# A selective-scan block on one core: norm statistics, softplus passes and the z product in other steps, and GpSimd's four B products at states 5, 7, 9, 11

## What is computed

```python
x = x + mamba(ln_channels(x))       # x: 4 x 512 x 24 x 24; pixel shuffle: 128 channels, 2304 positions
# inside, per image, after a projection to u, z (256 channels each), a causal 4-tap conv and silu on u:
dt, Bm, Cm = split(x_proj @ u);  dt = softplus(dt_proj @ dt + bias);  A = -exp(A_log)
h = exp(dt * A) * h + (dt * u) * B   # 256 channels x 16 states, one position after the other
y = sum_over_states(h * C) + u * D
y = out_proj @ (y * silu(z))
t = tokens(x)                        # then a layer norm over the 512 channels of each token (ln_t)
t = t + ffn(ln_t(t))                 # ffn: tokens 1..128 replaced by a routed mix of memory tokens
```

## Time and profile before

| | us |
|---|---|
| median of 3 runs | 1271.66 (1270.97 to 1273.31) |
| profiled execution, its own time | 1275.06 |
| its span, first to last instruction | 1273.2 |
| POOL busy | 1107.9 (87%) |
| PE busy | 1095.4 (86%) |
| DVE busy | 1088.3 (85%) |
| ACT busy | 874.4 (69%) |
| mean granted PE clock | 0.935 |

### The profile page before, as it was taken

One profiled execution on the slowest core, in us unless ns is written; L12 is line 12 of the kernel. 1 busy time (PEld: TensorE's weight loads), 2 busy tenths in 40 slices (PEclk: granted clock), 3 DMA queues, 4 the chain that ended last, 5 costly groups with the idle time before them and its releaser, 6 DMA issues.

```text
span 1273.2 us, 13359 instructions
## 1 busy us (share of the span) xinstructions
PE 1095.4 (86%) x3786; PEld 646.5 (51%) x3786; DVE 1088.3 (85%) x1269; ACT 874.4 (69%) x1628; POOL 1107.9 (87%) x753
## 2 busy tenths in 40 slices
PE   6578888898898898898988988988988988989797
PEld 4334554555555555455555555555555555555344
DVE  1298999998999999998998999999989999999772
ACT  2466777767767757767767767777668677687543
POOL 4188999998999999998999989999989999999763
PEclk8678999998999999998999989999989999999898
DMA  6221213212213212222213212222122132232561
GB/s 163 76 74 52 101 60 103 101 58 106 102 57 106 97 62 90 92 82 82 101 58 105 101 58 99 76 88 101 60 104 101 57 106 101 75 105 93 172 207 37
DMA packets 64539, 116.80 MB, mean 92 GB/s; under 512 B 34218, under 2 KB 47954, under 8 KB 64466
## 3 DMA queue, kind: packets, MB, share of 16 engines
...
## 4 chain that ended last, share of the span: by engine, by line
POOL 31%; PE 21%; issue 18%; ACT 17%; DVE 12%; POOLq 0%; DMA 0%; DVEq 0%; SPq 0%; ACTq 0%
POOL SCAN L427 18%; DVE SCAN L1008 9%; PE Yp L736 7%; POOL SCAN L439 7%; PE PP L891 4%; ACT DA L504 3%; POOL GZ L418 2%; DVE SCAN L968 2%; PE PP L819 2%; PE PP L871 2%; ACT GATES L618 2%; ACT GATES L537 2%; ACT GATES L534 2%; ACT GATES L619 1%; PE PP L864 1%
## 5 line engine op out<-in xcount | busy, mean ns | idle before, releaser
L1008 DVE TENSOR_TENSOR_SCAN SCAN<-DA,CAR,SCAN 128x384 f32<-128x384 f32 x768 | 728.7, 999 | 67.4 <-ACT DA L504 34.4
L427 POOL TENSOR_TENSOR SCAN<-SCAN,CS 128x768 f32<-128x768 f32 x384 | 692.6, 1820 | 36.6 <-DVE SCAN L1008 32.0
L736 PE MATMUL Yp<-SCAN,IDENT 128*128 128x384 f32 x1536 | 588.6, 510 | 54.8 <-DVE VV L979 38.5
L504 ACT ACTIVATE DA<-UDT,A 128x384 f32<-128x384 f32 x768 | 432.3, 578 | 218.6 <-DVE SCAN L1008 215.1
L736 PEld LDWEIGHTS Yp<-SCAN,IDENT 128*128 128x128 f32 x1536 | 288.9, 198 | 267.0 <-POOL SCAN L427 104.7
L968 DVE TENSOR_TENSOR SCAN<-UDT,BB 128x768 f32<-128x768 f32 x288 | 269.3, 935 | 34.8 <-PE BB L718 34.8
L439 POOL TENSOR_TENSOR SCAN<-UDT,BS 128x768 f32<-128x768 f32 x96 | 175.3, 1826 | 0.0
L891 PE MATMUL PP<-XN,WT 128*128 128x384 f32 x384 | 141.1, 503 | 0.0
L891 PEld LDWEIGHTS PP<-XN,WT 128*128 128x128 f32 x384 | 77.3, 202 | 56.7 <-issue 11.0
L718 PE MATMUL BB<-PT,SEL 96*128 96x384 bf16 x288 | 98.7, 343 | 2.4 <-DVE SCAN L968 2.3
L451 POOL TENSOR_TENSOR UDT<-UDT 128x768 f32<-128x768 f32 x24 | 43.5, 1812 | 48.3 <-DVE UDT L1085 48.3
...
## 6 DMA issues: line engine op xcount, KB each, us to landing
...
```

What stands on the lines that cost most here:

```text
L427: pool.tensor_tensor(M[:, n1 % MRING], HB[:, n1 % HRING], over_halves(CS[:, n1 % CRING]), ALU.mult).then_inc(m_ready, 1)
L504: act.activation(DA[:, h, 0:T], DT[:, par, h], ACT.Exp, scale=A[:, h, n:n + 1])\
L736: last = pe.matmul(Yp[:, h, 0:T], IDENT[:, :], M[:, n3 % MRING, h], start=n3 == 0, stop=n3 == NS - 1)
L1008: dve.tensor_tensor_scan(HB[:, s % HRING, h], DA[:, h, 0:T], HB[:, s % HRING, h], CAR[:, ds(J * NS * HALVES + s * HALVES + h, 1)], ALU.mul ...
```

## The change

It moves pieces to other steps, on five engines; no piece is added or dropped, no tile changes its size.

- GpSimd's driving terms are those of states 5, 7, 9, 11 in place of 3, 5, 7, 9. State 3 goes to PE and DVE, state 11 to POOL. The DMA that fills BS now waits for the last of POOL's four products of the unit before.
- Back norm: mean and XC2 from steps 9/10 to 6 (XC2 behind the scan of the step), square from 11 to 7, variance from 12 to 9, its Ln/Exp from 12 to 10, POOL's two instructions from 13/14 to 12/13.
- Norm of unit J+3: square from 11 to 10, variance from 12 to 11, Ln/Exp from 12 to 11.
- Softplus: Exp in step 7, Ln and Exp in 8, two squares in 9, Identity in 10, the other two squares in 11, and all of them behind the decays of their step.
- z: product from step 10 to 12 (in the units without norm it stays at 10), its two readings from 11 to 12, the clamp from 12 to 13. u*D (L742) from step 11 to 10.

```diff
-POOL_STATES = (3, 5, 7, 9)
+POOL_STATES = (5, 7, 9, 11)
...
                 sp.wait_ge(rows_written, 16 * (unit + 1))
+                positive(sp, dbu_pool, NPOOL * unit)
...
-                if main and s == 12:
+                if main and s == 13:
                     pool.wait_ge(sgz_chain, 2 * J + 1)
...
-                if front and s == 10:
-                    act.wait_ge(fac_chain, 3 * f + 2)
-                    act.activation(SS[:, :, :], SS[:, :, :], ACT.Square, bias=FITB[:, 2:3], scale=FIT_S)\
-                        .then_inc(fac1_square, 1)
...
                     act.activation(DT[:, fp], PPT, ACT.Relu).then_inc(relu_done, 1)
-                if front and s == 8:
                     act.wait_ge(sp_chain, 3 * f + 1)
                     act.activation(SE[:, :, :], SE[:, :, :], ACT.Exp, scale=-1.0).then_inc(sp_chain, 1)
+                if front and s == 8:
                     act.wait_ge(sp_chain, 3 * f + 2)
...
-                if main and s == 11:
+                if main and s == (12 if norm else 11):
                     act.wait_ge(z_ready, J + 1)
...
-                if back and s == 11:
+                if back and s == 7:
                     act.wait_ge(xc2_ready, k + 1)
...
-                if back and s == 9:
+                if back and s == 6:
                     pe.wait_ge(x2_ready, k + 1)
-                    if front:
-                        pe.wait_ge(relu_done, f + 1)
                     for q in range(Q):
                         last = pe.matmul(STAT2, MEANW[:, :], unit_x(k)[:, q], start=q == 0, stop=q == Q - 1)
...
+                if main and s == (12 if norm else 10):
+                    if back:
+                        pe.wait_ge(ln2_done, k + 1)
+                    if front:
+                        pe.wait_ge(relu_done, f + 1)
+                    if norm:
+                        pe.wait_ge(ln_done, g + 1)
...
                     pe.wait_ge(hi_ready, f + 1)
                     if back:
-                        pe.wait_ge(x2_ready, k + 1)
+                        pe.wait_ge(xc2_ready, k + 1)
```

102 lines of the change are left out of this document (49 added, 53 removed).

## The result

The changed kernel takes 1278.57 us (median of 6, 1277.19 to 1280.50) where the kernel before takes 1273.39 (6 runs, 1270.97 to 1276.27): a ratio of 1.0033, 95% interval 1.0017 to 1.0050 (the two medians by themselves give 1.0041). It is slower by a third of a percent; the forecast was 1252. The profiled execution took 1279.57 us, its span is 1277.8.

A forecast was written before the change was run, and what follows sets the result against it. No engine is full; a loop through DVE and POOL bounds the kernel. Legs 16.40 + 31.46 = 47.86, plus 0.25 for clock, gives 48.1 a unit; 14 us over 20 units plus the ends saves 19.3: 1252, range 1237 to 1270.

The forecast's parts named there:

- What bounds it: Whole unit: no engine is full; a loop through DVE and POOL sets the 48.7 us, with waits of order, not capacity.
- POOL's wait for dt: POOL ahead of dt*u: waits 1.99 us before the change, about 1.0 after; POOL isn't the bound.
- Leg A: DVE from scan 7 to the first softplus-ending instruction, ended by ACT's softplus chain: 16.40 us, 1.04 less than before.
- the four small waits: DVE at scans 9, 10, 11 and the first softplus-ending instruction: waits for ACT of 2.3 us in all.
- Leg B: DVE from the first softplus-ending instruction to the next scan 7: 31.46 us, where it was 31.00.
- XC2's wait: DVE at step 6: XC2 waits 0.95 us for PE's mean, a new wait on the loop.
- POOL's two back-norm instructions and the clamp change places within POOL's slack: POOL's steps 12 and 13: moving these instructions adds nothing to the unit's time.
- Clock: PE's half-clock stretches after long waits: cost 0 to 1.6 us a unit, taken as 0.25.
- Rival B: PE's wait ahead of the first Yp sum puts every x projection at half clock: 49.4 a unit, 1279 us; chance 0.10.
- The ends: Outside units 1 to 20: savings of 2.4 at the start, 2 in units 21 and 22, 0.9 in the last scan unit.
- The start: Start and unit 0: DVE's first product 1.5 us earlier, with unit 0's changes 2.4 us saved together.
- Units 21 and 22, without norm, save some 2 together: The two units near the end that have no norm: about 2 us less together.

The follow-up runs named there:

- e4: Changed kernel with DVE's XC2 behind the drive of state 8 instead of behind scan 6: 1259.63 us, 0.9894 of the kernel before.
- e8: Changed kernel with POOL's RSTD2 product behind dt*u, XC2 behind drive 8, z at step 11 in units without norm, and idle matmuls on PE: 1250.11 us, ratio 0.9811.
- e3: Changed kernel with z's product at step 11 instead of 10 in the units without norm: 1272.90 us, 0.9985 of the kernel before.

## Why the prediction was wrong

**What bounds it** held in the main: no engine is full, and the unit is the sum of DVE's two legs, with ACT's chain as the first. That POOL's wait for dt is slack did not; it is forced, and in e4 and e8 it is part of the bound. It was to shrink to some 1.0 us and stayed at 1.95, since L1080 now ends late.

**Leg A** (scan 7 to L1080) was forecast as 16.40 and measures 586.23 - 569.87 = 16.36. The sum over ACT's list was right, row by row, and the four small waits are where it had them: 1.14, 0.34 and 0.14 ahead of scans 9 to 11 and 0.31 at L1080, 1.93 in all, or 2.3 with the overlaps, as forecast. (Before the change DVE waits for POOL a third time in the unit, 0.73 ahead of scan 9. The forecast does not name it; it lies in this leg and drops out of the sum.)

**Leg B** was forecast as 31.46 and measures 48.31 - 16.36 = 31.95. XC2's wait is 0.55 and not 0.95, scan 6 waits 0.24 for its decay, which was not in the sum: together -0.16. The missing term is L1080's 0.72; 0.07 of the difference stays unassigned. The step that failed is one sentence, whose price in the sum is nothing: "POOL's two back-norm instructions and the clamp change places within POOL's slack". The places were costed on POOL alone; what the instruction does to DVE, which runs beside it, was not asked, though the trace of before had the 1.79 us row.

**Clock** was put at 0.25 us a unit and cost 48.67 - 48.31 = 0.36 on the average. The reason given for a low value was right in kind and too large: where half clock follows the wait of 2.12, the wait ahead of the next first Yp sum is 2.45 to 2.75, and where it doesn't, 3.40; it never falls to 2. Half clock follows five of these 20 waits, those of 2.70, 2.75 and 3.40 (three). The reading of before was off too: half clock follows its wait of 2.56 us in 19 of the units 1 to 20, not in some, and what sets the slow units apart is that it lasts twice as long there (0.50 from 590.2 to 596.9, where unit 9 has it from 542.4 to 545.7). Rival B has the sign and, by chance, the time (1279), but its mechanism is a small part: each x projection at half clock would cost 1.56 a unit, and five of 20 are, at 1.4 each. The Trainium skill's "TensorE: Matmul & The Clock Gate", section "HAM oscillation — how this bites in real kernels", describes the drop at every repetition, in a kernel that waits for DMAs between its bursts; here the trace shows it behind the wait ahead of the first Yp sum in five of 20 units, and behind the wait of 2.12 in 16.

Units 1 to 20 so miss by 11.6 us. The terms come to 11.2 of it: 0.72 x 20 = 14.4 for the hold, 2.2 for the clock (0.11 a unit), less 5.4 for the rest (0.16 + 0.07 of leg B and 0.04 of leg A, a unit).

**The ends** miss by 13 us, as much again. The start was right (-3.3 for -2.4). The second step that failed is "Units 21 and 22, without norm, save some 2 together", which was never worked out: z there kept its step and got a wait for an Ln that had moved behind ACT's squares; e3 shows that this alone is worth 5.7 us. The last stretch took z's wait for the same Ln as well, where the forecast had looked only at one broadcast; in e3 it is back at 95.2, as before the change. What remains there are units 21 and 22, 99.0 against 97.5 before and the 95.5 forecast; where that lies was not found.

**What the rows of before could have given** (an estimate): 47.86 + 0.72 for the hold is 48.6 at full clock, and with the five slow units that the kernel before has already, 48.9 a unit, no faster than before, and z's new wait on top.
